# A mixture-of-experts layer with its 18 experts worked on in pairs: three tiles of inner columns for two experts in place of four

## The reference

```python
def _L0_ffn_ref(hidden_states, gate_w, w_gate, w_up, w_down, sw_gate, sw_up, sw_down):
    E, K, I = (16, 4, 176)
    IS = 352
    CAP = 128
    ...
    scores = jax.nn.softmax(x @ gate_w.T, axis=-1)
    topk_w, topk_i = jax.lax.top_k(scores, K)
    topk_w = topk_w / (topk_w.sum(-1, keepdims=True) + 1e-20)
    ...
    gact = jax.nn.silu(jnp.einsum('ech,ehi->eci', xg, w_gate))
    mid = gact * jnp.einsum('ech,ehi->eci', xg, w_up)
    eout = jnp.einsum('eci,eih->ech', mid, w_down) * wbuf[..., None]
    ...
    shared = jax.nn.silu(x @ sw_gate) * (x @ sw_up) @ sw_down
    return (y + shared).reshape(b, s, h)
```

## Time and profile before

| | us |
|---|---|
| median of three runs | 1562.75 |
| profiled execution, its own time | 1562.25 |
| span of the profiled execution | 1559.7 |
| this layer, from the first load of weights to the last sum | 369.26 to 471.18 |
| PE busy over the whole span | 1391.5 (89%) |

### The profile page before, as it was taken

The page is one execution under the profiler, slowest core; times in us unless marked ns, Lnnn a source line. Parts: engine busy times, 40 slices in busy tenths (PEclk is TensorE's granted clock), DMA queues, the critical chain, the costliest instruction groups (busy, mean ns, idle before and its releaser), DMA issues. The chain is left out here.

```text
span 1559.7 us, 24153 instructions
## 1 busy us (share of the span) xinstructions
PE 1391.5 (89%) x8036; PEld 982.4 (63%) x8036; DVE 1096.3 (70%) x2242; ACT 862.0 (55%) x2296; POOL 576.4 (37%) x643
## 2 busy tenths in 40 slices
PE   7877989866999689987779899999998989999979
PEld 5653444444776347876557678788877446666657
DVE  4687999925666566764568776765654679999963
ACT  2446989932123354426445545545554589999931
POOL 2237777630000001530346325533500037777710
PEclk9986999967999799998889999999999999999989
DMA  4001545445340322300200000000001354334110
GB/s 148 1 1 24 93 96 95 93 150 156 116 151 0 82 62 67 84 1 1 78 5 14 14 14 2 14 1 1 1 1 46 131 162 122 101 104 122 41 55 13
DMA packets 126855, 96.11 MB, mean 62 GB/s; under 512 B 84697, under 2 KB 101081, under 8 KB 126092
## 3 DMA queue, kind: packets, MB, share of 16 engines
q1 hardware_dynamic: 126732, 94.58, 21.9%
HBM read 77.51 MB, written 0.26 MB: 50 GB/s over the span
## 5 line engine op out<-in xcount | busy, mean ns | idle before, releaser
L599 ACT ACTIVATE x_v_full<-banks,x_neg_max,x_q_scale 128x1024 uint8<-128x1024 f32 x128 | 153.1, 1201 | 13.1 <-PE banks L379 12.0
L706 DVE TENSOR_REDUCE x_row_max<-banks 128x1 f32<-128x512 f32 x248 | 151.9, 680 | 11.2 <-PE banks L379 10.9
L536 POOL CAST x_v_full<-x_v_full 128x1024 f16<-128x1024 uint8 x128 | 131.8, 1042 | 52.4 <-DMA x_v_full<-x_v_full 50.7
L212 PE MATMUL banks<-a_w_ring,x_normed_T 128*128 128x512 f32 x320 | 146.5, 598 | 4.8 <-DVE a_r L3225 4.8
L2704 DVE TENSOR_TENSOR ctx_tokens<-ctx_tokens,banks 128x512 f32<-128x512 f32 x128 | 87.7, 685 | 82.2 <-ACT x_weights_T L2590 60.3
L2422 PE MATMUL banks<-ctx_tokens,x_kT 128*128 128x512 f32 x272 | 140.1, 602 | 2.8 <-ACT ctx_tokens L2584 2.2
L2443 PEld LDWEIGHTS banks<-x_v,x_weights_T 128*128 128x128 f32 x896 | 113.0, 194 | 20.8 <-issue 17.5
L2443 PE MATMUL banks<-x_v,x_weights_T 128*128 128x129 f32 x896 | 118.1, 278 | 2.1 <-ACT x_weights_T L2600 2.1
L2538 POOL TENSOR_TENSOR ctx_tokens<-ctx_tokens 128x512 f32<-128x512 f32 (+1 forms) x48 | 65.9, 1372 | 141.4 <-DVE ctx_tokens L2684 141.4
L379 PE MATMUL banks<-x_kT_parts,x_qT_int 64*128 64x512 bf16 x512 | 104.7, 400 | 6.5 <-DVE x_row_max L706 4.3
L3115 POOL TENSOR_TENSOR a_rms<-a_rms,a_minus_half 128x4 f32<-128x4 f32 x64 | 64.9, 1014 | 115.7 <-ACT a_rms L3045 115.7
(11 more groups left out here) (530 smaller groups left out, 3304.3 us busy)
## 6 DMA issues: line engine op xcount, KB each, us to landing
a_w_ring<-in_L_attn_WB_T SPq DMA_DIRECT2D x16, 512.0 KB
a_w_ring<-in_L_attn_WC_T SPq DMA_DIRECT2D x16, 512.0 KB
f_w_gate_up<-in_L_ffn_gate_up SPq DMA_DIRECT2D x18, 352.0 KB
ctx_tokens<-in_ctx SPq DMA_DIRECT2D x16, 256.0 KB, 5.6
x_wq<-in_L_xattn_Wq_T SPq DMA_DIRECT2D x8, 512.0 KB, 3.8
a_w_ring<-in_L_attn_Wth_T SPq DMA_DIRECT2D x8, 512.0 KB
a_bias_ring<-in_L_attn_B_bias_perm SPq DMA_DIRECT2D x16, 256.0 KB
a_bias_ring<-in_L_attn_C_bias_perm SPq DMA_DIRECT2D x16, 256.0 KB
```

Source lines behind the costliest of these rows:

```text
L212: last = nc.tensor.matmul(out, lhsT, rhs, start=(i == 0), stop=(i == len(pairs) - 1))
L536: nc.gpsimd.tensor_copy(pf[:, q % RING], pt8[:, q % RING]).then_inc(s.unpacked, 1)
L599: nc.scalar.activation(eb[:, q % RING], k.ps[:, 2 + 2 * (q % 2):4 + 2 * (q % 2), :].rearrange("p a n -> p (a n)"), ACT.Exp, bias=nb[:, v % ...
L706: nc.vector.reduce_max(mx[:, u % 2, i:i + 1], k.bank(MBANK[m % 3]), AX.X).then_inc(s.max_taken, 1)
```

## The change

Two experts, 2n and 2n + 1, are worked on together as pair n. Of their 2 x 176 inner columns the first 128 of each make a tile of their own, and the remaining 48 of both share a third one, which has 112 columns (`TAIL`): 48 of the first, a gap of 16 columns of zeros, 48 of the second. So the second expert's rows begin at partition 64.

- Gate and up of a pair are 2 matrices x 3 tiles x 2 channel blocks = 12 matmuls, where two experts had 16. The third tile's gate and up share a bank.
- Down is as many matmuls as before, 4 for an expert, but in each batch the first contracts 128 rows and the second 48, which lie at partitions 0 to 47 or 64 to 111.
- ACT does two sigmoids for a pair (128x512 and 112x256), DVE four products in place of four, of which two have 512 columns and two have 256.
- PE's order is gate and up of pair n, then down(2n - 2) and down(2n - 1). The banks are 0 to 2 and 3 to 5 for gate and up, 6 and 7 for the outputs. The counts now lie in bank 7, which down(1) overwrites, so down(1) waits for a new signal `cap_ready` after `capacity`. The logits lie in bank 3, so gate and up of pair 1 wait for `exp_ready`.
- DVE takes two outputs and does 3 decode steps for each pair from the second on; after the last pair the order is take(14), take(15), three decode steps, take(16), take(17).
- SP's ring has 3 pairs; pair n is loaded once down(2n - 5) is done. A pair is two transfers, of 736 KB and 384 KB, where two experts had four, of 352 KB and 176 KB each. The weights are laid out for it outside the kernel.

```diff
-        wgu = sb("w_gate_up", [P, RING, DC, 2, INNER])
-        wd = sb("w_down", [IH, RING, 2, D])
-        mid = sb("mid", [IH, 2, 2, BT])
-        sig = sb("sig", [IH, 2, 2, BT])
+        wgu = sb("w_gate_up", [P, RP, DC, 2, 2 * P + TAIL])
+        wd = sb("w_down", [P, RP, 3, D])
+        mid = sb("mid", [P, 2, 3, BT])
...
+                for n in range(npair):
+                    if n >= RP:
+                        sp.wait_ge(s.out_in_psum, 2 * (n - RP + 1))
+                    sp.dma_start(wgu[:, n % RP], A["L0_ffn_gate_up"][n]).then_inc(ring_loaded[n % RP], 16)
+                    sp.dma_start(wd[:, n % RP], A["L0_ffn_down"][n]).then_inc(ring_loaded[n % RP], 16)
...
+                def gate_up(n):
+                    r = n % 2
+                    pe.wait_ge(ring_loaded[n % RP], 32 * (n // RP + 1))
+                    if n == 1:
+                        pe.wait_ge(s.exp_ready, B)
+                    if n >= 2:
+                        pe.wait_ge(s.mid_ready, n - 1)
+                    for j in range(2):
+                        for m in range(2):
+                            matmul_acc(nc, k.bank(3 * r + j, P, BT, m * BT), [(wgu[:, n % RP, c, j, m * P:(m + 1) * P], k.xt[:, c]) for c in range(DC)])
+                        last = matmul_acc(nc, k.bank(3 * r + 2, TAIL, BT, j * BT), [(wgu[:, n % RP, c, j, 2 * P:2 * P + TAIL], k.xt[:, c]) for c in range(DC)])
+                    last.then_inc(s.gu_in_psum, 1)
...
                 def down(e):
-                    pe.wait_ge(s.mid_ready, e + 1)
+                    n, i = divmod(e, 2)
+                    rows = slice(64 * i, 64 * i + INNER - P)
+                    pe.wait_ge(s.mid_ready, n + 1)
+                    if e == 1:
+                        pe.wait_ge(s.cap_ready, 1)
                     if e >= 2:
                         pe.wait_ge(s.out_taken, B * (e - 1))
                     for b in range(B):
-                        last = matmul_acc(nc, k.bank(4 + e % 2, P, D, b * D),
-                                          [(mid[:, e % 2, m, b * T:(b + 1) * T], wd[:, e % RING, m]) for m in range(2)])
+                        tokens = slice(b * T, (b + 1) * T)
+                        last = matmul_acc(nc, k.bank(OUT_BANK + i, P, D, b * D),
+                                          [(mid[:, n % 2, i, tokens], wd[:, n % RP, i]), (mid[rows, n % 2, 2, tokens], wd[rows, n % RP, 2])])
                     last.then_inc(s.out_in_psum, 1)
...
+                    nc.scalar.activation(mid[:, r, 0:2].rearrange("p a n -> p (a n)"), k.bank(3 * r), ACT.Sigmoid)
+                    nc.scalar.activation(mid[0:TAIL, r, 2], k.bank(3 * r + 2, TAIL, BT), ACT.Sigmoid).then_inc(s.sig_ready, 1)
...
+                    nc.vector.tensor_tensor(whole, whole, k.bank(3 * r), ALU.mult)
+                    link(nc.vector.tensor_tensor(tail, tail, k.bank(3 * r + 2, TAIL, BT), ALU.mult))
+                    nc.vector.tensor_tensor(whole, whole, k.bank(3 * r + 1), ALU.mult)
+                    nc.vector.tensor_tensor(tail, tail, k.bank(3 * r + 2, TAIL, BT, BT), ALU.mult).then_inc(s.mid_ready, 1)
+                    if n == 1:
+                        capacity()
+                    if n >= 1:
+                        take(2 * n - 2)
+                        take(2 * n - 1)
```

More of the change, by code:

```diff
@@ L876, in down @@
                     for b in range(B):
-                        last = matmul_acc(nc, k.bank(4 + e % 2, P, D, b * D),
-                                          [(mid[:, e % 2, m, b * T:(b + 1) * T], wd[:, e % RING, m]) for m in range(2)])
+                        tokens = slice(b * T, (b + 1) * T)
+                        last = matmul_acc(nc, k.bank(OUT_BANK + i, P, D, b * D),
+                                          [(mid[:, n % 2, i, tokens], wd[:, n % RP, i]), (mid[rows, n % 2, 2, tokens], wd[rows, n % RP, 2])])
                     last.then_inc(s.out_in_psum, 1)
[L880 to L889, removed]
-                        pe.wait_ge(s.sel_ready, 1)
[L892 to L895, removed]
+                for n in range(npair):
+                    gate_up(n)
+                    if n == 1:
+                        pe.wait_ge(s.sel_ready, 1)
+                        nc.tensor.matmul(k.bank(COUNT_BANK, P, EXPERTS), k.keep[:], sel[:, 0], start=True, stop=True)
+                        matmul_acc(nc, k.bank(COUNT_BANK, P, EXPERTS, EXPERTS), [(k.ones[:], sel[:, 0]), (k.keep[:], sel[:, 1])]).then_inc(s.count_ready, 1)
+                    if n >= 1:
+                        down(2 * n - 2)
+                        down(2 * n - 1)
+                down(ne - 2)
                 down(ne - 1)
@@ L901, in _ @@
                 for b in range(B):
[L902 removed]
+                    nc.scalar.activation(prob[:, b, 0:EXPERTS], k.bank(LOGIT_BANK, P, EXPERTS, b * EXPERTS), ACT.Exp, bias=sm[:, b, 0:1],
                                          accum_out=sm[:, b, 1:2]).then_inc(s.exp_ready, 1)
[L904 to L910, removed]
+                for n in range(npair):
+                    r = n % 2
+                    act.wait_ge(s.gu_in_psum, n + 1)
+                    if n >= 2:
+                        act.wait_ge(s.out_in_psum, 2 * (n - 1))
+                    nc.scalar.activation(mid[:, r, 0:2].rearrange("p a n -> p (a n)"), k.bank(3 * r), ACT.Sigmoid)
+                    nc.scalar.activation(mid[0:TAIL, r, 2], k.bank(3 * r + 2, TAIL, BT), ACT.Sigmoid).then_inc(s.sig_ready, 1)
+                    for q in range(2 * n - SQUARES, 2 * n - SQUARES + 2):
+                        if not 0 <= q < 8:
+                            continue
+                        c, j = divmod(q, 4)
                         sl = slice(j * 512, (j + 1) * 512)
@@ L986, in _ @@
                 steps = 8 * len(MATS)
[L987 to L994, removed]
-                        capacity()
[L996 to L999, removed]
+                for n in range(npair):
+                    r = n % 2
+                    dve.wait_ge(s.sig_ready, n + 1)
+                    whole, tail = mid[:, r, 0:2].rearrange("p a n -> p (a n)"), mid[0:TAIL, r, 2]
+                    nc.vector.tensor_tensor(whole, whole, k.bank(3 * r), ALU.mult)
+                    link(nc.vector.tensor_tensor(tail, tail, k.bank(3 * r + 2, TAIL, BT), ALU.mult))
+                    nc.vector.tensor_tensor(whole, whole, k.bank(3 * r + 1), ALU.mult)
+                    nc.vector.tensor_tensor(tail, tail, k.bank(3 * r + 2, TAIL, BT, BT), ALU.mult).then_inc(s.mid_ready, 1)
+                    if n == 1:
+                        capacity()
+                    if n >= 1:
+                        take(2 * n - 2)
+                        take(2 * n - 1)
+                    for m in range(steps * max(n - 1, 0) // (npair - 1), steps * n // (npair - 1)):
+                        decode(m)
+                take(ne - 2)
                 take(ne - 1)
```

40 lines of the change are left out of this document (24 added, 16 removed).

## The result

| | before | changed |
|---|---|---|
| median of 16 runs each | 1562.84 us | 1567.28 us |
| lowest, highest | 1557.87, 1564.56 | 1562.03, 1569.73 |
| span of the profiled execution | 1559.7 | 1567.9 |
| first load of the layer to its last sum | 101.9 | 105.8 |

The ratio is 1.0026, with a 95% interval of 1.0017 to 1.0035: 4.1 us slower by the ratio, 4.4 by the medians, where I had forecast 0.65 more and 1563.4. The time lies inside the range of 1555.5 to 1568, but past the 1565.9 from which I would have called it slower, and past the forecast's own bounds (1561 to 1566). A few executions, of the kernel before and of others alike, took 2700 us and more; they are left out of every number here.

What follows compares the result with a forecast made beforehand. PE was taken to set the layer's and the program's pace. The terms -15.55 + 13.8 + 2.0 + 1.0 - 0.6 = +0.65 us gave 1562.9, plus 0.5 for the median: 1563.4 us, range 1555.5 to 1568.

Steps and rivals of the forecast that it cites:

- Fewer matmuls: Gate and up on PE: 216 instructions in place of 288, 72 x 0.216 = 15.55 us less.
- the borders: Downs on PE: 36 round trips between 128 and 48 rows at 0.39 us, 13.8 us more.
- rows 3 and 4: Earlier profile rows where 3-row and 64-row matmuls stand beside full ones; gave 0.39 us for a round trip.
- the first: Rival for the downs: 48 rows cost nothing extra, 8.6 us a pair, 1549.6 us in all; chance 0.13.
- the third: Rival for the downs: each border costs 0.16 us, not 0.09; 5.0 us more, 1568.4 us; chance 0.11.
- borders without repeats: Rival for the downs: only the borders cost, 6.5 us in place of 13.8, 1556.1 us; chance 0.07.
- the tail that waits: Rival at downs: a tail waits until the matmul before has written its sums; 5.0 us more, 1568.4; chance 0.11.
- The first load: Layer start: first gate and up wait for 1.147 MB, not 541 KB; PE starts 2.0 us later.
- The wait for `cap_ready`: Before down(1): PE stands 1.0 us (bounds 0.5 and 1.7) until DVE finishes pair 1's products and capacity.
- The end: Last downs: PE's wait before the last down goes, 0.6 us less; the last sum still 1.1 us after PE.
- The clock: Layer start: the rise from 1.2 to 2.4 GHz comes as long after PE's start; 0, 1 us either way.
- The ring of three: Rival at weight loads: ring too short, PE waits in 6 pairs from pair 3; 10.8 us, 1574; chance 0.03.

Runs made afterwards that it cites:

- the grouped kernel: Changed kernel with counts one pair earlier and each pair's downs together, four 128-row matmuls, then four tails side by side in the array's halves: 1548.12 us, 0.9900.
- the wait filled: Changed kernel plus two float32 matmuls (four instructions) with unread output on PE just ahead of down(1)'s wait for cap_ready: 1564.64 us, 1.0011.
- the three profiled kernels with grouped tails: Changed kernel with early counts and grouped tails, 1548.12 us; also split first load and no decoding behind last pair, 1547.82; also last outputs in banks 3 and 4, 1544.13.
- the counts early: Changed kernel with token counts and capacity moved one pair earlier, after gate and up of pair 0: 1562.84 us, 1.0006.
- full tails: Changed kernel with each tail matmul contracting all 112 rows, the other expert's down rows set to zero, wait kept: 1549.91 us, 0.9919.
- the borders in the kernel before: Kernel before, expert by expert, only the column cut changed so each down contracts 128, 64, 128, 64 rows: 1573.85 us, 1.0079.
- the smaller edits at both ends: On early counts and grouped tails: separate semaphores for down weights, no decoding behind the last pair, last outputs in banks 3 and 4: 1544.13 us, 0.9877.

## Why the prediction was right, and where it was wrong

*The core.* Fewer matmuls, -15.55, and the borders, +13.8: together -1.75. In the profiled execution the layer grew by 3.85 us, and -1.8 is what remains for this core when the terms below are taken off. The spacing of 0.63 us for each two at a border, a pair in 10.2 us, and the border's price in a kernel expert by expert (0.79 us an expert, expected 0.78) all agree. That rows 3 and 4 could stand for 48 rows was right. The three rivals about other prices fell with the pair: 8.6 us would have been the first, over 10.6 the third, and borders without repeats give 0.52 us for each two and not 0.63.

*The range.* That it holds 1567.28 is luck. Its part above 1566 was there for the tail that waits, which didn't come; what filled it was the clock, for which I had no chance and 1 us. I gave 0.17 to a slower kernel, and a slower kernel it is.

*The first load.* Forecast +2.0, measured +1.4 (5.3 us from the issue to PE's start, 3.9 before). The bytes came at 378 to 412 GB/s, not at the 240 to 346 of the earlier trace rows. The 1.0 us from the last byte to PE's start stayed (1.147 MB had passed at 375.4, PE starts at 376.44), so larger pieces took nothing off it.

*The wait for `cap_ready`.* Forecast 1.0, measured 0.94 to 0.99. Its place and length were right, its price was not.

*The end.* PE's last wait is gone (0.6 forecast and measured); the last sum comes 0.9 us after PE's end, 1.1 before.

*The clock.* This is the step that failed. I set it to 0, with 1 us to either side, and looked for it only at the start. There, PE began 1.4 us later and the clock rose 5.5 us after it began and not 4.0, which is 0.75. That 0.75 belongs to the execution and isn't shown to belong to the change: the rise came 5.3 us after PE's start in the changed kernel's second profile and 2.9 to 6.2 us after it in the experiments, 2.9 in the grouped kernel with the very same first load. What I did not ask is whether a wait of 1.0 us on PE, between downs in which PE stands at each border, could make the clock fall; I priced the wait by its length. It fell for 6.8 us, and the interval between the two ring issues around it (396.78 and 409.78) is 13.0 us where 10.2 is the pace: 2.8, and 0.5 within down(1) ahead of it: 3.3 us. So the sum for the layer is -1.75 + 1.4 + 0.75 + 1.0 + 3.3 - 0.6 - 0.2 = 3.9, against 3.85. The next layer adds 1.3 (from the norm that opens it, 471.5, to the following one 36.4 us before, 37.7 after, in both profiled executions of the changed kernel), as the clock falls there too. Another 1.0 lies between that norm and the next (507.9 to 535.6 before); I didn't take it apart. What makes the clock fall where the next layer begins is not settled: it did in the changed kernel (twice), with the wait filled, and in the three profiled kernels with grouped tails; it did not with the counts early, nor with full tails, nor with the borders in the kernel before.

*The ring of three* never mattered: PE did not wait for it.

## What to carry to other kernels

Count borders, not only matmuls: when a contraction of few rows (3, 48 and 64 here) stands between full ones of 128, each way costs 0.2 us, nearly a whole matmul instruction of 256 columns. By the medians, padding the thin ones with zero rows turned 4 us lost into 12 us gained; standing them side by side in the two halves of the array, with the counts moved, made it 14, and with the smaller edits at both ends 18. And a wait of PE in a thinly loaded stretch is priced by what the clock does behind it: move what it waits for, or fill it.

## What the runs showed that I had not expected

- A wait of 1.53 us between full matmuls left the clock at 1.00; one of 0.94 us between downs with borders brought it to 0.50 for 6.8 us, in two executions of two.
- Four matmul instructions of work that nobody reads, in the place of the wait, spared 6.8 us at half the clock: 3.1 us of the layer, 2.3 to 2.6 of the whole kernel.
- The rise of the clock at the layer's start came anywhere from 2.9 to 6.2 us after PE's start, which is worth up to 1.6 us between executions.
- The first loads passed at 378 to 412 GB/s in the changed kernel, where a contiguous piece of the gate and up weights is 5888 bytes long (one partition's share), and at 240 to 346 before, where it is 2816. The length alone doesn't settle it: with the borders in the kernel before the pieces are 2816 bytes too, and from 370 to 376 us 274 to 384 GB/s passed. There the down weights lie over 128 partitions, as in the changed kernel, and before over 88. No run sets the two apart. The changed kernel's rows:

```profile
373.00:374.00 1.00, 0.03 (x1) 0.00 (x0) 0.57 (x4) 0.19 (x2) 0.92 (x2) 0.50 0.98 406
374.00:375.00 1.00, 0.00 (x0) 0.00 (x0) 0.50 (x2) 0.98 (x5) 1.00 (x1) 0.50 0.94 378
```
